# Two row blocks of a graph product taking turns chunk by chunk, with the weight-side products moved to two banks of PSUM

## The reference

```python
bw  = sign(weight)                 # -1, 0, 1
ba  = maximum(sign(x), 0)          # 0 or 1
xw  = ba @ bw.T                    # 8192 x 256, small integers
out = layernorm(x + relu(adj @ xw), axis=-1)
```

## Time and profile before

| | |
|---|---|
| median of 3 runs | 995.71 us |
| the profiled execution's own time | 995.31 us |
| its span (first to last instruction) | 993.5 us |
| mean granted TensorE clock | 0.998 of 2.4 GHz |
| TensorE matmuls busy | 971.5 us, 98% |
| VectorE busy | 844.5 us, 85% |
| GpSimd busy | 842.0 us, 85% |
| ScalarE busy | 613.2 us, 62% |
| DMA, bytes moved and mean rate | 294.67 MB, 297 GB/s |

### The profile page before, as it was taken

The page is one execution under the profiler, slowest core; times in us unless marked ns, Lnnn a source line. Parts: engine busy times, 40 slices in busy tenths (PEclk is TensorE's granted clock), DMA queues, the critical chain, the costliest instruction groups (busy, mean ns, idle before and its releaser), DMA issues.

```text
span 993.5 us, 12241 instructions
## 1 busy us (share of the span) xinstructions
PE 971.5 (98%) x4484; PEld 802.0 (81%) x4484; DVE 844.5 (85%) x874; ACT 613.2 (62%) x655; POOL 842.0 (85%) x361
## 2 busy tenths in 40 slices
PE   5999999999999999999999999999999999999996
PEld 3788888888888888888888888888888888888885
DVE  4868998989888898988989898898988889898893
ACT  3777675665656566565665656566565666656562
POOL 2666998998889889898998889899888988989893
PEclk9999999999999999999999999999999999999999
DMA  9999999999999999999999999999999999999961
GB/s 281 348 337 332 325 308 334 271 315 287 330 300 289 317 286 319 291 304 311 285 311 295 325 291 296 304 299 314 293 319 297 295 290 316 314 277 329 296 194 40
DMA packets 298459, 294.67 MB, mean 297 GB/s; under 512 B 9376, under 2 KB 298400, under 8 KB 298400
## 3 DMA queue, kind: packets, MB, share of 16 engines
q1 hardware_dynamic: 157792, 155.47, 57.3%
q10 hardware_dynamic: 140608, 138.43, 49.5%
HBM read 285.47 MB, written 8.39 MB: 296 GB/s over the span
## 4 chain that ended last, share of the span: by engine, by line
PE 95%; DMA 3%; SPq 0%; DVE 0%; ACT 0%; POOL 0%; issue 0%; ACTq 0%
PE ps L501 93%; DMA x_sb<-in_x_dram 1%; PE ps L526 1%; DMA raw<-in_adj_dram 1%; PE ps L486 1%; PE ps L476 0%; POOL lo L249 0%; SPq L172 0%; DVE stats L381 0%; SPq L165 0%; DVE rows L377 0%; ACT hi L269 0%; ACT relu L278 0%; ACT rows L286 0%; DVE mv L384 0%
## 5 line engine op out<-in xcount | busy, mean ns | idle before, releaser
L249 POOL TENSOR_TENSOR lo<-turned,hi 128x1024 fp32r<-128x1024 f32 x352 | 840.9, 2411 | 134.7 <-ACT hi L269 130.6
L501 PE MATMUL ps<-hi,xw 128*128 128x512 f32 x2048 | 801.5, 391 | 3.7 <-POOL lo L249 1.9
L501 PE MATMUL ps<-lo,xw 128*128 128x512 f32 x2048 | 798.1, 390 | 0.0
L269 ACT ACTIVATE hi<-turned 128x1024 fp32r<-128x1024 f32 x352 | 373.3, 1061 | 257.1 <-PE ps L501 175.2
L501 PEld LDWEIGHTS ps<-hi,xw 128*128 128x128 f32 x2048 | 385.0, 188 | 84.5 <-ACT xw L262 3.7
L501 PEld LDWEIGHTS ps<-lo,xw 128*128 128x128 f32 x2048 | 385.1, 188 | 79.1
L369 DVE STREAM_TRANSPOSE turned<-raw 128x1024 f32<-128x1024 f32 x352 | 426.3, 1218 | 0.9 <-DMA raw<-in_adj_dram 0.9
L373 DVE TENSOR_TENSOR lo<-ps,hi 128x1024 fp32r<-128x1024 f32 x160 | 195.1, 1220 | 106.0 <-ACT hi L269 105.8
L269 ACT ACTIVATE hi<-ps 128x1024 fp32r<-128x1024 f32 x160 | 163.9, 1024 | 92.5 <-PE ps L501 76.9
L369 DVE STREAM_TRANSPOSE ps<-raw 128x1024 f32<-128x1024 f32 x160 | 194.9, 1218 | 4.1 <-DMA raw<-in_adj_dram 4.1
L286 ACT ACTIVATE rows<-rows,shift,rstd 128x256 f32<-128x256 f32 x62 | 36.2, 586 | 0.0
(11 more groups left out here) (25 smaller groups left out, 42.2 us busy)
## 6 DMA issues: line engine op xcount, KB each, us to landing
raw<-in_adj_dram ACTq DMA_DIRECT2D x254, 512.0 KB, 12.1
raw<-in_adj_dram SPq DMA_DIRECT2D x254, 512.0 KB, 11.0
rows<-in_x_dram SPq DMA_DIRECT2D x16, 512.0 KB, 10.5
out_dram<-rows SPq DMA_DIRECT2D x15, 512.0 KB, 15.8
x_sb<-in_x_dram ACTq DMA_DIRECT2D x14, 256.0 KB, 12.3
x_sb<-in_x_dram SPq DMA_DIRECT2D x14, 256.0 KB, 11.4
raw<-in_adj_dram ACTq DMA_DIRECT2D x4, 256.0 KB, 8.5
raw<-in_adj_dram SPq DMA_DIRECT2D x4, 256.0 KB, 9.0
```

The lines of the kernel that those rows point to most:

```text
L249: pool.tensor_tensor(lo[:, n % RING], turned[:, ordinal(n) % TP], hi[:, n % RING].bitcast(f32), ALU.subtract).then_inc(p_los_made, 1)
L269: act.activation(hi[:, n % RING], src, ACT.Copy).then_inc(his_made, 1)
L501: return pe.matmul(acc[b % 2][a], xw[:, step, a * P:(a + 1) * P], part[:, n % RING, k * MB:(k + 1) * MB], start=(step == 0 and part is hi) ...
```

## The change

Blocks 0 and 1 are worked on together: chunk c of block 0, then chunk c of block 1, then chunk c+1 of block 0, and so on; from unit 64 on the order is as before. Both pairs of accumulator banks are therefore in use from the start, and the products and transposes of the weight side move to banks 6 and 7: `ps_xw` takes both, the transposes use bank 6 (group 1 alone uses bank 2). So `turn_step(g)` now waits for the copy of group g-1, and `turn_step` and `make_xw`, which stood side by side, now stand at units of their own (`TURN_AT`, `MAKE_AT`). For groups 4 on, with the odd group g = 2c+1 and the even group g = 2c:

| after unit (TensorE) | operation | after hi of unit (ScalarE) | operation |
|---|---|---|---|
| 8c-6 | `turn_step(2c)` | 8c-5 | `cast(2c)` |
| 8c-4 | `make_xw(2c)` | 8c-1 | `copy_xw(2c)`, `cast(2c+1)` |
| 8c-2 | `turn_step(2c+1)` | | |
| 8c | `make_xw(2c+1)` | 8c+2 | `copy_xw(2c+1)` |

The step functions on VectorE stand 3 turns behind their `turn_step`. Units 8c and 8c+1 need group 2c, units 8c+2 and 8c+3 group 2c+1; units 8c+4 to 8c+7 are block 1's and use both again. The first groups have places of their own: `make_xw(1)` after unit 0; `turn_step(2)` after 5, `make_xw(2)` after 6, `turn_step(3)` after 7, `make_xw(3)` after 8, and on ScalarE `copy_xw(0)` behind hi(0), `copy_xw(1)` behind hi(2), `cast(2)` behind hi(6), `copy_xw(2)` behind hi(7), `cast(3)` behind hi(8) and `copy_xw(3)` behind hi(10).

The cast of group 1 moves from VectorE to GpSimd, the copy of group 0 from VectorE to ScalarE. `rows` gets a second buffer. The rows of `x` of chunk 1 are issued after chunk 1 of the new order (which is block 1's chunk 0) and not before it. The ending of block 1 starts 10 units after that of block 0.

```diff
+    ORDER = [(b, c) for c in range(CH) for b in range(2)] + [(b, c) for b in range(2, NBLK) for c in range(CH)]
+    PAIR = 2 * UB
+    END = [max(n for n in range(UNITS) if ORDER[n // UPC][0] == b) + 1 for b in range(NBLK)]
+    WORK = [END[0], END[0] + 10] + END[2:]
...
+    TURN_AT, MAKE_AT, NEED_AT = {}, {1: 0}, {}
+    for g in range(GROUPS):
+        NEED_AT[g] = 2 * UPC * (g // UPG) + g % UPG * UPG
+        if g >= 2:
+            TURN_AT[g] = NEED_AT[g] - (6 if g % 2 == 0 else 4)
+            MAKE_AT[g] = NEED_AT[g] - (4 if g % 2 == 0 else 2)
+    TURN_AT.update({2: 5, 3: 7})
+    MAKE_AT.update({2: 6, 3: 8})
...
-        rows = sb("rows", [P, MT, D], f32)
+        rows = [sb(f"rows{i}", [P, MT, D], f32) for i in range(2)]
...
-        ps_xw = ps[:, 2 * BANK:4 * BANK].rearrange("p (k d) -> p k d", k=GK)
-        ps_xT = [ps[:, b * BANK:(b + 1) * BANK].bitcast(bf16).rearrange("p (k a n) -> p k a n", k=GK, a=DH)
-                 for b in (6, 7)]
+        ps_xw = ps[:, 6 * BANK:8 * BANK].rearrange("p (k d) -> p k d", k=GK)
+        ps_xT = [ps[:, (2 if g == 1 else 6) * BANK:(3 if g == 1 else 7) * BANK].bitcast(bf16)
+                 .rearrange("p (k a n) -> p k a n", k=GK, a=DH) for g in range(GROUPS)]
...
+        def rows_of(b):
+            return rows[(min(b, NBLK - 1) + 1) % 2]
...
-                              adj_v[ch // CH, ch % CH, g]).then_inc(adj_loaded[ch % SLOTS], 16)
+                              adj_v[ORDER[ch][0], ORDER[ch][1], g]).then_inc(adj_loaded[ch % SLOTS], 16)
...
-            early = 4 + 2 * half if ch < CH else max(CH + 3 - ch, 0) + half
-            return max(UPC * (ch - SLOTS + 1) + early, 0)
+            early = UPC + 1 + half if ch < 2 * CH else max(2 * CH + 3 - ch, 0) + half
+            return UPC * (ch - SLOTS + 1) + early
         def x_at(c, half):
-            return max(UPC * c - 9 + 2 * half, 0)
+            return 2 * UPC * (c - 1) - 5 + half if c > 1 else 0
+        def starts_at(n):
+            return any(n in (issue_at(ch, half), x_at(min(ch, CH - 1), half))
+                       for ch in range(1, 2 * CH) for half in range(2) if ch > 1 or n == 0)
+        def start_due(eng, n, side):
+            if n == 0:
+                start_chunk(eng, 1, side[1:2])
+            for c in range(1, CH):
+                for half in range(2):
+                    if n == x_at(c, half):
+                        start_x(eng, c + 1, side[half:half + 1])
+            for ch in range(2, 2 * CH):
+                for half in range(2):
+                    if n == issue_at(ch, half):
+                        start_chunk(eng, ch, side[half:half + 1])
...
+            start_chunk(sp, 1, LOWER[0:1])
+            for n in range(PAIR):
+                if starts_at(n):
+                    sp.wait_ge(units_turned, n + 1)
+                    start_due(sp, n, LOWER)
+            load_rows(0)
+            for ch in range(2 * CH, NCHUNK):
+                sp.wait_ge(units_turned, (ch - SLOTS + 1) * UPC)
+                start_chunk(sp, ch, LOWER)
+                for b in range(NBLK):
+                    if b < NBLK - 1 and ch == -(-(WORK[b] + 26) // UPC) + SLOTS - 1:
+                        store_rows(b)
+                    if b == 1 and ch == 2 * CH + 3 or b >= 2 and ch == max(b * CH + 7, 3 * CH + 2):
+                        load_rows(b)
...
+            pool.wait_ge(x_loaded[1], G * 16)
+            pool.tensor_copy(cast_x[:, 1], x_sb[:, GK:2 * GK]).then_inc(second_cast, 1)
...
-                        act.wait_ge(units_used, (b + 1) * UB)
+                        act.wait_ge(units_used, END[b])
...
-            start_x(act, 2, UPPER)
-            start_chunk(act, 1, UPPER)
+            start_chunk(act, 1, UPPER[0:1])
...
+                for g in range(GROUPS):
+                    if n == (0 if g == 0 else MAKE_AT[g] + (1 if g == 2 else 2 if g % 2 else 3)):
+                        copy_xw(g)
+                    if g >= 2 and n == TURN_AT[g] + 1:
+                        cast(g)
+                start_due(act, n, UPPER)
...
-                if n < UB:
-                    g = n // UPG
-                    if n % UPG and g >= 1:
-                        copy_xw(g)
-                    if n % UPG and g + 2 < GROUPS:
-                        cast(g + 2)
-                else:
-                    ending(n // UB - 1, n % UB)
+                for b in range(NBLK - 1):
+                    ending(b, n - WORK[b])
...
-            first_cast(0)
+            dve.wait_ge(x_loaded[0], G * 16)
+            dve.tensor_copy(cast_x[:, 0], x_sb[:, 0:GK]).then_inc(first_cast, 1)
             dve.wait_ge(signs_turned, 1)
             dve.tensor_copy(sign_wT[:], ps_wT).then_inc(signs_copied, 1)
             make_step(0)
-            dve.wait_ge(xw_made, 1)
-            dve.tensor_copy(xw[:, 0:GK], ps_xw).then_inc(xw_copied, 1)
             for n in range(UNITS):
                 turn(n)
-                if n == 0:
-                    first_cast(1)
                 if n and kinds[n - 1] == "V":
                     make_lo(n - 1)
-                g = n // UPG
-                if n < UB and n % UPG == 0 and g % 2:
-                    make_step(g)
-                if n < UB and n % UPC == UPC - 1 and g + 1 < GROUPS:
-                    make_step(g + 1)
-                if n >= UB:
-                    ending(n // UB - 1, n % UB)
...
+                for g in range(1, GROUPS):
+                    if n == (1 if g == 1 else TURN_AT[g] + 2 if g <= 3 else TURN_AT[g] + 3):
+                        make_step(g)
+                for b in range(NBLK - 1):
+                    ending(b, n - WORK[b])
...
-                if n < STEP_BUFS:
-                    pe.wait_ge(first_casts, n + 1)
+                if n == 0:
+                    pe.wait_ge(first_cast, 1)
+                elif n == 1:
+                    pe.wait_ge(second_cast, 1)
                 else:
                     pe.wait_ge(casts_made, n - STEP_BUFS + 1)
-                if n >= 2:
-                    pe.wait_ge(steps_made, n - 1)
+                    pe.wait_ge(xw_copied, n)
                 for k in range(GK):
                     for i in range(DH):
-                        last = pe.transpose(ps_xT[n % 2][:, k, i], cast_x[:, n % STEP_BUFS, k, i * P:(i + 1) * P],
+                        last = pe.transpose(ps_xT[n][:, k, i], cast_x[:, n % STEP_BUFS, k, i * P:(i + 1) * P],
...
-                b, u = n // UB, n % UB
+                b, c = ORDER[n // UPC]
+                u = c * UPC + n % UPC
...
-                if n < UB and n % UPG == 0:
-                    g = n // UPG
-                    if g + 1 < GROUPS:
-                        make_xw(g + 1)
-                    if g + 2 < GROUPS:
-                        turn_step(g + 2)
-                if n >= UB and n % UB == BACK_AT:
-                    turn_back(n // UB - 1)
+                for g in range(1, GROUPS):
+                    if n == MAKE_AT[g]:
+                        make_xw(g)
+                    if g >= 2 and n == TURN_AT[g]:
+                        turn_step(g)
+                for b in range(NBLK - 1):
+                    if n == WORK[b] + BACK_AT:
+                        turn_back(b)
```

More of the change, by code:

```diff
@@ L93, in build @@
         warm = sb("warm", [P, 1], f32)
-        flat = [t.rearrange("p a b -> p (a b)") for t in (relu[:], rows[:])]
+        flat = [t.rearrange("p a b -> p (a b)") for t in (relu[:], rows[0][:])]
         cast_x = flat[0].bitcast(bf16).rearrange("p (s k d) -> p s k d", s=STEP_BUFS, k=GK)
@@ L124, in build @@
         signs_copied = sem("signs_copied")
-        first_casts = sem("first_casts")
+        first_cast = sem("first_cast")
+        second_cast = sem("second_cast")
         casts_made = sem("casts_made")
@@ L189, in _ @@
                 start_half(sp, i, LOWER)
[L191 to L195, removed]
             def store_rows(b):
                 sp.wait_ge(blocks_done, b + 1)
-                sp.dma_start(out_rows[b], rows[:]).then_inc(rows_stored, 16)
+                sp.dma_start(out_rows[b], rows_of(b)[:]).then_inc(rows_stored, 16)
             def load_rows(b):
-                if b == 0:
+                if b == 1:
                     sp.wait_ge(xw_made, GROUPS)
-                else:
[L206 to L224, removed]
+                elif b >= 2:
+                    sp.wait_ge(rows_stored, (b - 1) * 16)
+                sp.dma_start(rows_of(b)[:], x_rows[b]).then_inc(rows_loaded, 16)
+            start_chunk(sp, 1, LOWER[0:1])
[12 more added lines that the diff above has]
+                        load_rows(b)
             store_rows(NBLK - 2)
-            load_rows(NBLK - 1)
             for b, ms in PIECES:
@@ L232, in _ @@
                 sp.dma_start(out_rows[NBLK - 1, :, ms[0]:ms[-1] + 1],
-                             rows[:, ms[0]:ms[-1] + 1]).then_inc(rows_stored, 16)
+                             rows_of(b)[:, ms[0]:ms[-1] + 1]).then_inc(rows_stored, 16)
             sp.wait_ge(rows_stored, (NBLK - 1 + len(PIECES)) * 16)
```

(14 more changed lines are left out.)

6 lines of the change are left out of this document (1 added, 5 removed).

## The result

The changed kernel is slower: 1.0093 times the kernel before, with an interval of 1.0077 to 1.0109, by runs of 1004.33 and 1005.28 us against 995.21 to 995.80. The profiled execution took 1005.28 us, 9.97 more than that of the kernel before; 1003.3 was forecast, range 995 to 1007.

A forecast was written before the change was run, and what follows sets the result against it. TensorE was taken to bound the kernel from 36.00 us on, the loads before that. 0.15 + 6.65 + 1.2 = +8.0 us on the profiled 995.31 gave 1003.3; own range 1000 to 1005, full range 995.0 to 1007.0.

The forecast's parts named there:

- Part 1: Start up to unit 8: earlier loads are used up by two stalls of 2.4 us; +0.15 us.
- Part 2: Units 8 to 63: TensorE waits for copy, hi and lo at units 8c+3 and some 8c+4; +6.65 us.
- what waits behind the waiting ScalarE is hi and a cast: Units 8 to 63: only hi(8c+3) and cast(2c+2) stand behind the waiting copy; the cast ends before it is wanted.
- the pairs ask for less than the DMAs deliver: Later loads: chunk pairs ask for 290 GB/s, less than the 347 delivered; they cost nothing.
- 7 turns ahead of its use, as before: Later loads: a chunk is issued as far ahead of its use as in the kernel before; no cost.
- Part 3: Split pairs from unit 8 on: 13 more returns to the large matmuls at 0.09 us each; +1.2 us.
- A: Rival, whole kernel: only loads bound the start, hi and lo keep ahead of TensorE; faster, 992.5 us; chance 0.14.
- B: Rival, units 8 on: start as forecast, but no stall later; 996.7 us; chance 0.12.
- C: Rival, start: chunk 1 lands no sooner, unit 4 at 29.0, all 3 us later; 1006.3 us; chance 0.07.
- D: Rival, start: GpSimd's first cast ends late, unit 8 is 3.0 us late; 1006.3 us; chance 0.05.
- The endings: Units 64 to 95: two endings instead of one still fit on VectorE; costs nothing, up to 4 us once if not.

The follow-up runs named there:

- Experiment 4: Changed kernel with the rows of x of chunk 1 issued ahead of chunk 1 again; ratio 1.0122 to the kernel before.
- experiment 5: Experiment 3 plus, on ScalarE, cast(3) behind hi(7) and copy_xw(2) behind hi(8); ratio 1.0008 to the kernel before, profiled execution 996.58 us.
- experiment 2: Changed kernel with ScalarE issuing a unit's due DMAs right behind its hi, ahead of copy and cast; ratio 1.0078 to the kernel before, profiled execution 1003.71 us.
- Experiment 3: Changed kernel with DMAs ahead of copies and the odd groups' copy (from 3 on) behind hi(8c+3); ratio 1.0013 to the kernel before, profiled execution 996.71 us.
- experiment 7: Changed kernel with VectorE making lo at units 0, 3, 7, 11 and 14 modulo 16, so at every 8c+3; ratio 1.0095 to the kernel before.
- experiments 9: Kernel before with turn_step(g+2) moved behind unit 2g+1, splitting 14 pairs of small-matmul groups; ratio 1.0038 to the kernel before, profiled execution 999.47 us.

## Why the prediction was right, and what it missed

The direction, the mechanism and the range held. The profiled execution took 1005.28 us against a forecast of 1003.3, just above the forecast's own 1000 to 1005 (the other run compared, 1004.33, is inside) and inside the full range. The 2.0 us too few are late DMAs (1.5) and slow restarts (1.0), which had no term, less 0.6 us of terms taken too large. Point by point:

- **Part 1, +0.15.** Unit 8 was forecast at 38.45 and came at 38.39; chunk 1 at 22.3 (22.4), unit 4 at 26.0 (26.07), unit 5 at 28.45 (28.44), unit 6 at 30.9 (30.80), `turn_step(3)` at 36.85 (36.81). The first product came at 14.81 and not at 15.1, the cast taking 1.04 us in place of 1.2. So `make_xw(1)` came at 17.82 (forecast 18.6) and unit 3 at 23.85 (24.3); it did not matter, since chunk 1 sets unit 4. A gap of 0.49 us ahead of unit 7 was not forecast, and it only shortened the one ahead of `turn_step(3)` to 0.82. Experiment 4 shows that the earlier chunk is worth 3 us or more at unit 8, experiment 5 that the chain ahead of unit 8 costs 2.0.
- **Part 2, +6.65.** The gaps at 8c+3 were 0.58 to 0.61, six times, and 1.0 at unit 59 (forecast 0.62 and 1.05), those at 8c+4 0.39 to 0.42 (forecast 0.47): 4.6 + 1.6 = 6.2. The step from experiment 2 to 3 removes all of them but 0.11 at unit 12, and changes the place of one copy and nothing else; experiment 7 shows that GpSimd's lo is the last leg of the path. Of the 0.45 too much, 0.2 lies at 8c+3 and 0.25 at 8c+4.
- **What part 2 left out.** First, "what waits behind the waiting ScalarE is hi and a cast": its DMA issues wait too. That cost gaps of 0.61 at units 24 and 40, and about 0.15 ahead of units 23 and 39: 1.5 us. Experiment 2 gained 1.6 us in all and 2.0 from unit 8 on. The sentence of the prediction that the pairs ask for less than the DMAs deliver, hence cost nothing, was right on the rate and wrong on the time of issue. "7 turns ahead of its use, as before" is not exact either: by the code the two halves of a chunk's DMAs were due 8 and 6 turns ahead and are now due 7 and 6 ahead. Second, the restarts. Experiment 3 removes 8.7 us, and the gaps are 7.7 of them; the other 1.0 is what the restarts add. Behind a `turn_step` a wait adds little to a restart (0.34 against 0.31), behind a product about 0.1.
- **Part 3, +1.2.** The size is near by luck, the explanation only half right. Experiment 3 has all of the splits and next to no waits. It needs 122.6 us where the same work took about 121.5 before (131.3 less 9.8, which is the whole difference less the start's 0.1): 1.1 us. The prediction charged a slow restart of 0.09 for each split and overlooked that a `make_xw` with no `turn_step` behind it takes 0.80 and not 0.88. A split costs 0.04 to 0.055 (experiments 9 and 3), so 13 of them cost 0.5 to 0.7. Most of the rest lies in units 8 to 15 of experiment 3: from 38.54 to 56.37 they take 17.83 us where each of the next five rounds of eight takes 17.49. The 0.34 holds the slow restarts at units 8 and 12 and the gap of 0.11.
- **The sum.** 0.1 start + 6.2 gaps + 1.5 late DMAs + 1.0 restarts + 1.1 = 9.9; measured 9.97. The last two terms are remainders, the 1.0 of experiment 3's 8.7 and the 1.1 of the whole, so the sum closes by construction. Measured by themselves are the start, the gaps, the 8.7 and, of the 1.1, the 0.8 to 1.0 told above.
- **The rivals.** A and B fell with the gaps. C fell with the turn at 22.43 (experiment 4 is what C would look like). D fell with the cast: it starts at 12.51, within 0.1 us of the landing of its rows (3.73 + 8.7 = 12.4), and takes 1.04. The Trainium skill ("GPSIMD Engine Reference", "Instruction dispatch") states that the first call to a freshly loaded kernel costs about 6 us more; no such time is seen here ahead of the cast, GpSimd's first.
- **The endings.** Two in units 64 to 95 and the second `rows` buffer cost nothing: TensorE is busy for all of 824.70 us in the last stretch.

## What to carry to other kernels

When an operation that waits for TensorE is put into another engine's list, add up the path behind it in that list (here copy, hi, GpSimd's lo: 5.6 us) and compare it with TensorE's own work until it wants the result (5.0). The 0.6 us at each round of eight units, with the backlog behind them, were 6.2 of the 10 us lost, and moving the operation behind one more independent one removed all but 0.1 of them. DMA issues are members of that list too. And a gain ahead of a point that a load sets is no gain: ask which landing comes next.

## What was not expected of the hardware

- After a wait the second 512-column product starts 0.30 to 0.34 us behind the first, where 0.23 is usual, even when no other kind of matmul stood between (48.24 and 48.58 at unit 12). Behind a small matmul it is 0.31 without a wait.
- 8 matmuls of 256 columns followed by 512-column ones take 0.80 us from first start to next start (40.30 to 41.10), followed by transposes 0.88 (48.04 to 48.92 in the kernel before).
